# Queries and keys by seven block products instead of eight, all of them ahead of the attention loop

## What is computed

```python
h = _layernorm(x, axis=-1) * (1 + ca) + sa
q = (x @ Wq + bq).reshape(b, h, t, dh)          # b, h = 4, 16; t = 512, dh = 128
k = (x @ Wk + bk).reshape(b, t, h, dh).transpose(0, 2, 3, 1)
v = (x @ Wv + bv).reshape(b, t, h, dh).transpose(0, 2, 1, 3)
logits = jnp.einsum('bhtd,bhds->bhts', q, k) * scale
weights = jax.nn.softmax(logits + mask, axis=-1)
out = jnp.einsum('bhts,bhsd->bhtd', weights, v)
return out.transpose(0, 2, 1, 3).reshape(b, t, h * dh) @ Wo + bo
```

## Time and profile before

| | us |
|---|---|
| median of 3 runs (lowest, highest) | 1694.1 (1689.21, 1695.77) |
| the profiled execution | 1690.27 |
| its span, first to last instruction | 1688.4 |
| TensorE busy | 1590.7 (94%) |
| VectorE busy | 898.1 (53%) |
| ScalarE busy | 697.6 (41%) |
| GpSimd busy | 602.6 (36%) |
| DMA engines, mean share | 43% |

### The profile page before, as it was taken

One profiled execution on the slowest core, in us unless ns is written; L12 is line 12 of the kernel. 1 busy time (PEld: TensorE's weight loads), 2 busy tenths in 40 slices (PEclk: granted clock), 3 DMA queues, 4 the chain that ended last, 5 costly groups with the idle time before them and its releaser, 6 DMA issues.

```text
span 1688.4 us, 29975 instructions
## 1 busy us (share of the span) xinstructions
PE 1590.7 (94%) x9012; PEld 1379.2 (82%) x9013; DVE 898.1 (53%) x2102; ACT 697.6 (41%) x1689; POOL 602.6 (36%) x641
## 2 busy tenths in 40 slices
PE   6999989999999999999999999868998799999997
PEld 3888578888888888888888888767887688888896
DVE  4323136666656566666666565877565322222267
ACT  4222155555555555555555555431231123232232
POOL 0001034554554535545445445744215111111143
PEclk9999999999999999999999999998998999999998
DMA  7522225243343344342524334584212344665555
GB/s 262 197 109 103 88 71 162 80 126 107 98 136 87 94 129 123 100 124 62 161 84 125 108 91 120 182 289 174 62 56 107 148 176 178 219 228 195 180 184 179
DMA packets 178453, 232.42 MB, mean 138 GB/s; under 512 B 78600, under 2 KB 137352, under 8 KB 175328
## 3 DMA queue, kind: packets, MB, share of 16 engines
q1 hardware_dynamic: 168112, 204.76, 37.1%
q0 software_dynamic: 5680, 18.62, 3.8%
q10 hardware_dynamic: 4608, 8.39, 1.5%
HBM read 151.72 MB, written 80.00 MB: 137 GB/s over the span
## 4 chain that ended last, share of the span: by engine, by line
PE 76%; DVE 9%; DMA 7%; ACT 3%; issue 3%; POOL 1%; SPq 1%; POOLq 0%; ACTq 0%; DVEq 0%
PE bank L1117 45%; PE bank L1194 9%; PE bank L1275 7%; PE bank L1229 7%; DMA slot_results<-y_sb 6%; PE bank L1258 4%; PE bank L1130 1%; PE bank L1326 1%; PE bank L1352 1%; DVE o_lo L1595 1%; DVE pt_lo L1593 1%; ACT o_hi L971 1%; DVE h L1760 1%; POOL tile_hot L799 1%; DVE ht_lo L1778 1%
## 5 line engine op out<-in xcount | busy, mean ns | idle before, releaser
L1117 PE MATMUL bank<-w,xt_hi 128*128 (+2 forms) x1136 | 286.4, 334 | 17.7 <-issue 8.0
L938 ACT ACTIVATE prob<-bank,neg_max 128x128 f32<-128x128 f32 (+3 forms) x256 | 134.2, 526 | 237.9 <-DVE neg_max L1634 235.4
L1117 PEld LDWEIGHTS bank<-w,xt_hi 128*128 128x128 f32 x1136 | 198.8, 192 | 30.7 <-issue 26.2
L679 POOL CAST q_hi<-q_raw 128x512 fp32r<-128x512 f32 x64 | 71.0, 1109 | 383.9 <-PE bank L1229 235.4
L1117 PE MATMUL bank<-w,xt_lo 128*128 (+2 forms) x568 | 185.9, 327 | 0.0
L1117 PE MATMUL bank<-w,ht_hi 128*128 (+3 forms) x426 | 143.1, 417 | 22.2 <-DVE ht_lo L1778 22.1
L1778 DVE TENSOR_TENSOR ht_lo<-bank,ht_hi 128x128 fp32r<-128x128 f32 (+1 forms) x213 | 48.4, 282 | 213.9 <-ACT ht_hi L1051 213.8
L1117 PE MATMUL bank<-wv_hi,h_lo 128*128 128x256 f32 x512 | 144.6, 282 | 0.0
L1117 PE MATMUL bank<-wv_lo,h_hi 128*128 128x256 f32 x512 | 144.4, 282 | 0.0
L1117 PE MATMUL bank<-wv_hi,h_hi 128*128 128x256 f32 x512 | 144.2, 282 | 0.0
L950 ACT ACTIVATE prob<-prob,row_inv 128x128 f32<-128x128 f32 (+3 forms) x256 | 136.3, 557 | 1.4
(11 more groups left out here) (192 smaller groups left out, 4045.8 us busy)
## 6 DMA issues: line engine op xcount, KB each, us to landing
ch_raw<-wexp SPq DMA_DIRECT2D x128, 170.0 KB, 2.7
experts_hi<-ch_hi SPq DMA_DIRECT2D x128, 170.0 KB, 2.0
experts_lo<-ch_lo SPq DMA_DIRECT2D x128, 170.0 KB, 2.2
w<-experts_hi SPq DMA_DIRECT2D x10, 2176.0 KB, 8.7
w<-experts_lo SPq DMA_DIRECT2D x10, 2176.0 KB, 15.2
q_transposed<-q_out SPq DMA_DIRECT2D x64, 256.0 KB, 2.0
q_raw<-q_transposed SPq DMA_DIRECT2D x32, 512.0 KB, 4.4
slot_results<-y_sb SPq DMA_DIRECT2D x39, 256.0 KB, 2.0
```

The costliest lines, as they stand in the source:

```text
L679: pool.tensor_copy(hi, raw).then_inc(split_hi, 1)
L938: ins = act.activation(prob[:, h, ROW_AT[r]:ROW_AT[r] + (r + 1) * P], bank[2 + i % 2][:, at:at + (r + 1) * P], ACT.Exp, bias=neg_max[:, h, ...
L1117: ins = pe.matmul(dst, a, m, start=(k == 0), stop=(k == last))
```

## The change

**Seven products.** For a pair of heads and a pair of batches the 12-matmul products form a two by two block product whose inner dimension is also cut in two (feature chunks 0, 1 and 2, 3). It was eight block products of 6 matmuls. It is now seven (Winograd's form), with sums of weight blocks (`sums` on GpSimd into `s_raw`), sums of input blocks (`t_sums` on VectorE, split in two parts by `t_high` and `t_low`), and sums of the results on VectorE (`total`). A unit is a pair of heads of queries or keys; a half is a unit with two of the four batches, 42 matmuls in `half(v)` on TensorE. There are 14 units and 28 halves. The first four query heads keep the plain form (`plain(b)`: 4 heads of 12 matmuls for each batch), and lie around `half(0)`.

**Keys to DRAM.** All 16 key heads are made ahead of the loop, split in two parts in a ring of three buffers (`k_ring`) and stored to `k_d`; a piece is 512 KB, four to a half. In the loop each step loads the next keys (1 MB) into `k_even` or `k_odd`. The splits of key weights leave GpSimd's list in the loop, `k_part` leaves ScalarE's and VectorE's.

**The loop's lists.** The first two parts of the scores of the next step move up into this step, around `weigh`; `values(0)`, `values(1)` open a step; values and transposes are interleaved; `pt_hi`, `pt_lo` have a buffer for each head. GpSimd splits the second head's queries after two expert pieces, not before four.

The core of the diff:

```diff
+UNITS = [("q", 2), ("q", 3), ("k", 0), ("q", 4), ("k", 1), ("q", 5), ("k", 2), ("q", 6), ("k", 3), ("q", 7),
...
+def stage1_order(plain, half):
+
+    plain(0)
+    plain(1)
+    half(0)
+    plain(2)
+    plain(3)
+    for v in range(1, NV):
+        half(v)
...
+        k_d = dram("keys", (NIT, P, 2, 2, T))
...
+                    for k, (done, count, b, h) in enumerate(((k22_ok, kv + 1, b1, 1), (kl_ok, 3 * kv + 1, b0, 0),
+                                                             (kl_ok, 3 * kv + 2, b1, 0), (kl_ok, 3 * kv + 3, b0, 1))):
+                        e = (4 * kv + k) % 3
+                        sp.wait_ge(done, count)
+                        sp.dma_start(k_d[pair * B + b, :, :, h, :], ring[e].bitcast(F32)).then_inc(k_st[e], 16)
...
                 if not last:
+                    if not first:
+                        sp.wait_ge(s_full, n * 6)
+                        load_k(n + 1, (b + 1) % 2)
                     sp.wait_ge(q_ok, n * 2 + 2)
                     load_q(p if b < B - 1 else p + 1, (b + 1) % B)
...
+                pool.tensor_tensor(s_raw[:, 0], w21, w22, ALU.add).then_inc(sum_ok, 1)
+                pool.tensor_tensor(s_raw[:, 2], w11, w21, ALU.subtract).then_inc(sum_ok, 1)
...
+                        pool.tensor_tensor(ring[e][:, 1, :], src, ring[e][:, 0, :].bitcast(F32),
+                                           ALU.subtract).then_inc(kl_ok, 1)
...
+                        if n >= 3:
+                            act.wait_ge(k_st[n % 3], 16 * (n // 3))
...
+                        act.wait_ge(half_ok, sum_count(v, done))
+                        act.activation(ring[n % 3][:, 0, :], src, ACT.Copy).then_inc(kh_ok, 1)
...
+                pe.wait_ge(ul_ok, 2 * i + 1)
+                product(0, plain_w(0, 0), rows(0))
+                pe.wait_ge(ul_ok, 2 * i + 2)
+                t_ready(1)
+                product(1, sum_w(1), t_rows(2))
+                t_ready(2)
+                product(2, sum_w(2), t_rows(3))
+                t_ready(4)
+                product(3, sum_w(0), t_rows(1))
+                if v == 0:
+                    for j in range(TT):
+                        transposes(2, j)
+                product(4, plain_w(2, 0), rows(2))
+                product(5, sum_w(3), rows(DC + 2))
+                product(6, plain_w(2, 1), t_rows(4))
...
-                def next_keys(h, chunks):
-                    if not last:
-                        keys(n + 1, p if b < B - 1 else p + 1, (b + 1) % B, h, chunks)
...
+                    values(0)
+                    values(1)
+                here, there = b % 2, (b + 1) % 2
+                scores(2, n, here)
                 project(0)
                 project(1)
-                scores(2)
+                scores(3, n, here)
                 project(2)
-                scores(3)
+                scores(4, n, here)
                 project(3)
...
+                scores(5, n, here)
+                turn(0, (0, 1))
                 if not first:
                     values(2)
+                turn(0, (2,))
+                if not first:
                     values(3)
-                turn(0, (0, 1))
-                next_keys(0, range(DC))
-                turn(0, (2,))
-                next_keys(1, (0,))
+                turn(1, (0, 1))
+                if not last:
+                    scores(0, n + 1, there)
                 weigh(0)
-                turn(1, (0, 1))
-                next_keys(1, range(1, DC - 1))
                 turn(1, (2,))
+                if not last:
+                    scores(1, n + 1, there)
+                if not first:
+                    pe.wait_ge(wo_add, n * TT)
                 weigh(1)
-                next_keys(1, (DC - 1,))
...
+                dve.wait_ge(e1_ok, v + 1)
+                dve.tensor_tensor(g_s, p6, e1_s, ALU.add).then_inc(half_ok, 1)
+                dve.tensor_tensor(w_s, p7, g_s, ALU.add).then_inc(half_ok, 1)
+                dve.tensor_tensor(u_s, p5, g_s, ALU.add).then_inc(half_ok, 1)
+                total(d22, p5, bb, w_s)
...
+                total(d11, p2, ba, e1_s)
...
+                total(d12, p3, ba, u_s)
...
+                total(d21, p4, bb, w_s)
```

More of the change, by code:

```diff
@@ L399, in adaln_layer @@
         ids_ok = sem("slot_tokens_ok")
-        g_ld = [sem(f"g_ld{i}") for i in range(NT)]
+        g_ld = [sem(f"g_ld{i}") for i in range(TT)]
         f_w1 = sem("f_w1")
@@ L514, in load_q, with stored, load_k @@
+            def stored(e, halves):
+                return len([k for k in range(4 * halves) if k % 3 == e])
             def load_q(p, b):
                 sp.dma_start(q_raw[:, :, :], q_v[:, b, :, bass.ds(p * 64, 64)]).then_inc(q_ld, 16)
-            load_q(0, 0)
+            def load_k(n, s):
+                sp.dma_start(k_both[s][:, :, :, :].bitcast(F32).rearrange("p k h t -> p (k h t)").unsqueeze(1),
+                             k_v[:, bass.ds(n, 1), :]).then_inc(k_ld[s], 16)
+            stage1_order(plain, half)
@@ L519, in _ @@
+            stage1_over(sp)
+            for e in range(3):
+                sp.wait_ge(k_st[e], 16 * stored(e, NK))
+            load_k(1, 1)
+            sp.wait_ge(h_ld, 32)
+            load_h(1)
+            sp.dma_start(wo_raw[:, :, :], wo_v[:, 0:2, :]).then_inc(wo_ld, 16)
             for s in range(2):
@@ L922, in bias_rows @@
+            stage1_order(plain, half)
+            stage1_over(act)
             def bias_rows(b):
@@ L1007, in step @@
                     load_xin(1, 1, 1)
-                for g in range(3):
-                    pt_part(1, g)
+                pt_part(1, 2)
+                if not last:
+                    exps(1, n + 1)
+                    normalise(0, n + 1)
                 o_part(1)
-                if not last:
-                    k_part(pn, n + 1, 1)
             def load_xin(m, s, tile):
@@ L1582, in _ @@
-            with dve.Fori(1, B) as b:
-                batch(b)
-            for m in range(2, 6):
-                mod_piece(m)
+                h_low(0, i)
+            stats(1)
+            stats(2)
+            normalise(1)
+            hidden(1, 0)
+            hidden(1, 2)
+            for i in range(TT):
+                h_low(1, i)
+            t_sums(0)
+            unit_low(0)
+            sums_low(0)
+            t_low(0, (2, 3, 4))
+            normalise(2)
+            dve.wait_ge(const_ld, 5 * 16)
@@ L1588, in _, with plain @@
+            def plain(b):
+                if b == 2:
+                    hidden(3, 0)
+                    hidden(3, 2)
+                    for i in range(TT):
+                        h_low(3, i)
+                    t_sums(1)
+                    t_low(1, (2, 3, 4))
+                if b % 2:
+                    t_low(b // 2, (1,))
+            stage1_order(plain, half)
             stage1_over(dve)
@@ L1651, in pt_part @@
                     cols = slice(PT_AT[g], PT_AT[g] + PT_LEN[g])
-                    low(pt_lo[:, cols], bank[4 + g % 2][:, 0:PT_LEN[g]], pt_hi[:, cols], None, pt_ok)
+                    low(pt_lo[:, h, cols], bank[4 + g % 2][:, 0:PT_LEN[g]], pt_hi[:, h, cols], None, pt_ok)
                 def o_part(h):
```

1009 lines of the change are left out of this document (617 added, 392 removed).

## The result

The changed kernel takes 1730.1 us (median; 1728.5 to 1731.4) against 1692.7 for the kernel before in the same comparison: a ratio of 1.022 (1.020 to 1.025), 2.2% slower. The forecast was 1697, with a range up to 1726, so the time lies outside it. The profiled execution has a span of 1727.6 us, 39.2 above that of before.

The account below looks back on a forecast made before the run. TensorE's own stream was taken as the bound in stage 1 and loop. +136.5 + 10 - 9 - 134 + 2 = +5.5 on the profiled 1690.3 gave 1695.8, median some 1699.6; forecast 1697 between them, range 1655 to 1726.

Parts of the forecast that it names:

- Stage 1: Before the loop: 600 more matmuls on TensorE, +136.5 us, all else beside the halves hidden; +10 for its start.
- The waits of the start: Start of stage 1: TensorE waits around the transposes of batches 1 to 3, +10 us (+3 to +18).
- The ring's rival: Key halves: stores over 4.7 us hold the ring, 1.7 us a half, +27 us, 1723; 12%.
- The first step: First keys through second step's keys: 48 key matmuls, 10.9 us, leave; 2 given back; -9 us (-5 to -11).
- The loop: 30 steps, each falling from 27.26 to 22.8 us: -134 us.
- the walk: One loop step summed link by link across engines: 22.8 us (22.5 to 23.1); total 1687 to 1709, 45%.
- the three waits: TensorE in each loop step: 1.1 us at `weigh(1)`'s third group, 0.3 at projection, 0.3 at last two transposes.
- TensorE's own list: One loop step: TensorE's work without the new waits, 21.1 us.
- longer steps: Loop: steps of 23.6 us, each of about 25 links 0.05 later; +24 us, 1721; 13%.
- The last two steps: End: last step and tail cost +2 us (0 to +6); table predicts -2.7 for last two steps and all behind.
- TensorE stays the bound: Loop: links quicker than summed, a step of 21.2 to 22.0 us, about 1660 (1648 to 1673); 27%.
- The clock: Loop: waits grown to 2.65 us halve TensorE's clock, up to 1.6 us a step; +48 us, 1745; 3%.

Follow-up runs that it names:

- the fill alone: Changed kernel with four loads later in SyncE's list, plus 41 unread TensorE matmuls in its first step: ratio 1.0184.
- the kernel without waits: Changed kernel with five edits: one-column `neg_max`, later loads, `pt_lo` third part before first output, queries loaded before keys, second head's `o_hi` earlier: 1657.3 us, ratio 0.9810.
- two edits: Each alone in the changed kernel: third part of `pt_lo` ahead of first head's output, 1.0213; second head's `o_hi` ahead of exponential and `normalise`, 1.0188.

## Why the prediction was wrong

**Stage 1: right.** +146.5 predicted, +147.1 measured. With eight products it is 35.0 us longer, so TensorE does bound it, as the sum had it. The waits of the start are 1.1, 1.9, 2.0, 0.5 and 1.6 us at the places named, plus three of 1.0 at the modulation rows that I hadn't named: TensorE is idle 10.1 us of the stage, and I took 10. The ring's rival did not decide there either: a key store lands in 3.0 us, under the 4.7.

**The ring, at one place.** I cost the loads of the next step at nothing ("most of a step ahead") and never looked at what the *first* of them were queued ahead of. They stand before the stores that free the ring: 6.5 us, by the run that moved them. The rival had the right mechanism (ScalarE waits for the DMA of `keys`, then TensorE for a bank) but the wrong cause and place: once, not 1.7 in each key half.

**The first step: the failed step of the prediction, -9 became +8.9.** It is "48 key matmuls, 10.9 us, leave it. The softmax there has nothing else beside it, so I give 2 back". It counted TensorE's work in a stretch that, with this work gone, is a chain through ScalarE, GpSimd and VectorE. By the traces, from the last matmul of stage 1 to the first exponential is 15.0 us before and 19.9 after, and from there to the first `o_hi` 17.3 and 21.2:

- Ahead of the exponential, 24 of the key matmuls (5.7 us) did leave the chain. In their place stand the last key pieces on ScalarE and GpSimd: the first `v_hi` comes 13.9 us after the end of stage 1, and 6.5 of these are the loads, as the run that moved them shows. Behind it ScalarE has two bias rows of 1.8 us each and a table load of 1.3 before its first exponential. These lay beside other work before; now they are in the chain. A second chain is as long: GpSimd splits the first queries behind its last key piece, TensorE waits 3.6 us for that, and the first `neg_max` ends 0.2 us before the exponential starts.
- Behind the exponential, about 3 of the 3.9 us are the next step's first mask, maxima, `neg_max` (1.1 us long here) and exponentials, which the new order puts ahead of `o_hi`. This is an estimate, the sum of these rows; with the one-column `neg_max` the stretch is 1.1 us shorter. Here also lies the half clock, 1.8 us or more. The other two bias rows lie here too, but they were in the chain before the change as well; without them the first `o_hi` is 2.7 us earlier than with the fill alone.

The loads and the clock have runs of their own. The split of the rest is read from the traces, and no run took it apart.

**The loop: right mechanism, sizes too small.** I had 21.1 of TensorE and 1.7 of waits, 22.8. Against the kernel without waits, at 21.41 a step, the starts of the matmuls give for the changed kernel 1.4 us at the third group of `weigh(1)`, 0.37 at the projection, 0.17 at the transposes, and the rest, 0.2, mostly behind them at half clock: 23.6. So the walk had the three waits in their places, at 1.1, 0.3 and 0.3. What failed are two sizes: TensorE's own list (21.1, measured 21.4) and the `neg_max` in the first wait. The table hides 3 us of the miss of the loop, since 27.26 stood for a mean of 27.38. The half clock I had priced at nothing for waits up to 1.1 us. In two of these steps the values behind a wait of 2.0 or 1.6 us are at half clock; the first:

```profile
484.67 0.39 PE L1580 MATMUL bank<-pt_hi,v_hi 128*128 128x256 f32 x1 [2.02 <-DVE pt_lo L1989]
...
485.29 0.42 PE L1376 MATMUL bank<-wv_lo,h_hi 128*128 128x256 f32 x1
485.50 0.41 PE L1376 MATMUL bank<-wv_hi,h_lo 128*128 128x256 f32 x1
```

**What the walk had missed.** It took `neg_max` at the 0.17 of one step. That row was the short form of an instruction that can be nine times as long; its longest row before, 1.5 us, was there to be seen. Without the hold the step is 22.94. That the walk's 22.8 is near it is in part luck, since its list is 0.3 short. The experiments on the order confirm that the waits are a round, where moving one link moves the wait.

**Two sums that don't come out.** The walk's upper bound is "each link in the walk 0.05 later; there are about 25". That is 1.25 us and a step of 24.0, not 23.6, and the case *longer steps* would have been 30 x 1.2 = 37 us slower, some 1734, with the measured time under it. And 7.2 less 0.69 and 1.57 is 4.9, not the 4.7 at which the ring was to decide, which changes nothing.

**The last two steps** came out 1.1 us longer, where they and all behind them were to give 2.7. In the run with small key loads the last step is 3.0 us shorter, with `q_raw` landing in 4.8 and not 7.0, so the key loads that I costed at nothing do cost something there. The 6.3 us behind the last step are not explained.

**The rivals.** *TensorE stays the bound* was not this kernel, but it is the one with five edits, at 21.41 us inside the 21.2 to 22.0 given. *Longer steps* at 23.6 is what the loop did, but not by links that were each 0.05 later. *The clock* showed in two stretches of 5 us of the loop, at 0.66 each, and in the ten behind the first `o_hi`, at 0.85 and 0.81: TensorE lost 5 us of its pace by that, not 48.

## What to carry to other kernels

A stretch in which one engine is always busy tells nothing of the chain under it: before work is taken out of it, the chain must be walked as if that engine were free. When a change makes the bound engine's list shorter, the order of the other engines' lists, which cost nothing until then, becomes the bound, and it has to be changed as a round. Of two edits here one gave 1 us alone and the other 6, neither clear of the intervals; with the first one, the shorter `neg_max` and the later loads in place, the second gave 39. For every duration on the path take its longest row too, not one step's. And where two traces are cut at an instruction, look at what the change moved across it.

## What the runs showed of the hardware

`neg_max` on two columns in SBUF (128x2, a VectorE instruction with one source) is 0.17 us, or up to 1.48 in the changed kernel when GpSimd is at work (2.26 in the run with `o_hi` of the second head moved alone), and all 33 long rows end within 0.03 us of a GpSimd instruction's end; on one column it is 0.14 to 0.16 in every row of every run. Two one-column instructions in its place, 0.21 us together, took 15 us off the changed kernel and 6 off the one before. The Trainium skill, "SBUF — State Buffer", "SBUF: two separate sides", says that VectorE in a two-port mode and GpSimd hold a shared pair of ports for a whole instruction each, and that the other blocks; the rows agree. The Trainium skill, "VectorE: DVE Perf Modes", "What auto-detection actually checks", gives that mode to an instruction with one source whose source and destination lie in SBUF with an outermost dimension over one that is even (or equal in both). Two columns have one, a single column has none; the two forms in the trace part in the same way. Shape and place are not enough, though: the reciprocal `row_inv` of the same shape stayed at 0.17 us in all 64 rows, 20 of them inside a GpSimd instruction. Which other operations are held was not looked into.

A wait costs TensorE more than the view lists: 0.8 us of listed waits a step cost 1.4, because each is counted from the end of a matmul of 0.39 us that the next follows after 0.23, and because the second matmul behind a wait starts 0.1 us later than in a stream. In the first step TensorE at half clock (0.50 granted, 1.2 GHz) for 20 us cost 1.8 us or more, not the half of that time, because most of the chain ran through other engines.
